# Linear-attention layers reordered: centring folded into TensorE, queries and first feed-forward product split in fp32r, second one in fp32

## What is computed

```python
q = _phi((h @ wq + bq_).reshape(b, s, H, DH))          # _phi(t) = elu(t) + 1, 16 heads of 8
k = _phi((h @ wk + bk_).reshape(b, s, H, DH))
v = (h @ wv + bv_).reshape(b, s, H, DH)
kv = jnp.einsum('bshd,bshm->bhdm', k, v)
z = 1.0 / (jnp.einsum('bshd,bhd->bsh', q, k.sum(axis=1)) + 1e-06)
att = jnp.einsum('bshd,bhdm,bsh->bshm', q, kv, z).reshape(b, s, d)
h = _ln(h + att @ wo + bo_, g1_, be1_)
y = jax.nn.gelu(h @ w1 + c1_, approximate=False) @ w2 + c2_
return _ln(h + y, g2_, be2_)
```

## Time and profile before

| | |
|---|---|
| median of 3 runs | 2228.36 us (2226.25 to 2234.08) |
| the profiled execution | 2234.25 us, span 2232.5 us |
| busy in the span | PE 1889.7 us (85%), DVE 1437.7 (64%), ACT 1330.7 (60%), POOL 533.2 (24%) |
| mean granted TensorE clock | 0.929 of full |
| one layer of stage B | 72.56 us: PE busy 67.57, DVE 38.50, ACT 41.26 |

### The profile page before, as it was taken

How to read it: one execution, slowest core, us unless ns; L and a number is a source line. 1 busy time by engine, 2 the same in 40 slices (tenths; PEclk the granted TensorE clock), 3 DMA queues, 4 the chain that set the end, 5 groups by cost and what they waited for, 6 DMA issues and landing times.

```text
span 2232.5 us, 23751 instructions
## 1 busy us (share of the span) xinstructions
PE 1889.7 (85%) x8305; PEld 1065.8 (48%) x8324; DVE 1437.7 (64%) x2318; ACT 1330.7 (60%) x2118; POOL 533.2 (24%) x525
## 2 busy tenths in 40 slices
PE   8899999999999989899677777997677677777998
PEld 6687444444434437686223233784122222332686
DVE  6687554465445646786755563786899755653787
ACT  6698646465555558797355556555654545565554
POOL 1344000000000001444411113122499501113121
PEclk9899999999999999899779998998799868999899
DMA  2431000000000003321000000210000000000110
GB/s 72 81 76 51 15 17 17 0 17 17 17 0 17 9 10 57 69 69 44 1 1 1 1 1 1 72 34 0 9 4 30 1 1 1 1 1 1 48 57 19
DMA packets 60610, 52.39 MB, mean 23 GB/s; under 512 B 2336, under 2 KB 55968, under 8 KB 60512
## 3 DMA queue, kind: packets, MB, share of 16 engines
q1 hardware_dynamic: 60512, 51.12, 8.9%
HBM read 49.47 MB, written 1.64 MB: 23 GB/s over the span
## 4 chain that ended last, share of the span: by engine, by line
PE 54%; DVE 22%; ACT 15%; issue 5%; DMA 2%; POOL 1%; SPq 0%; ACTq 0%; DVEq 0%; POOLq 0%
PE ps L440 8%; PE ps L442 8%; PE ps L441 8%; PE ps L708 5%; DVE arena L1439 4%; PE ps L225 4%; DVE arena L1184 4%; PE ps L701 4%; PE ps L927 3%; ACT arena L1047 2%; PE ps L897 2%; ACT rstd L242 2%; ACT arena L997 2%; ACT rstd L238 2%; PE ps L886 2%
## 5 line engine op out<-in xcount | busy, mean ns | idle before, releaser
L548 DVE TENSOR_TENSOR hid_lo<-arena,hid_hi 128x512 fp32r<-128x512 f32 x384 | 340.0, 897 | 72.2 <-ACT arena L498 70.2
L1184 DVE TENSOR_REDUCE arena<-ps 128x1 f32<-128x512 f32 (+3 forms) x352 | 214.0, 639 | 90.2 <-PE ps L901 87.4
L526 POOL TENSOR_TENSOR w_lo<-wslot,w_hi 128x512 fp32r<-128x512 f32 x56 | 76.7, 1374 | 787.8 <-DVE w_hi L543 787.8
L1104 POOL TENSOR_SCALAR_AFFINE_SELECT arena<-arena 128x256 f32<-128x256 f32 x256 | 102.5, 406 | 465.4 <-ACT arena L1047 462.8
L440 PE MATMUL ps<-x_hi,w_hi 128*128 128x512 f32 x512 | 208.7, 408 | 2.9 <-POOL w_lo L526 2.2
L441 PE MATMUL ps<-x_lo,w_hi 128*128 128x512 f32 x512 | 205.5, 401 | 0.0
L442 PE MATMUL ps<-x_hi,w_lo 128*128 128x512 f32 x512 | 205.2, 401 | 0.0
L495 ACT ACTIVATE hid_hi<-ps,wslot 128x512 fp32r<-128x512 f32 x256 | 177.1, 692 | 44.9 <-PE ps L442 17.7
L1047 ACT ACTIVATE arena<-ps 128x1024 f32<-128x1024 f32 (+3 forms) x256 | 166.3, 705 | 46.6 <-PE ps L917 45.9
L897 PE MATMUL ps<-arena 128*128 128x128 bf16 (+3 forms) x498 | 134.2, 336 | 63.5 <-DVE arena L1184 35.8
L498 ACT ACTIVATE arena<-ps,wslot 128x512 f32<-128x512 f32 x256 | 175.1, 684 | 16.8 <-DVE hid_lo L548 16.8
(11 more groups left out here) (223 smaller groups left out, 3876.7 us busy)
## 6 DMA issues: line engine op xcount, KB each, us to landing
arena<-gates_dram SPq DMA_DIRECT2D x96, 256.0 KB, 5.1
wslot<-pack_a SPq DMA_DIRECT2D x16, 514.5 KB, 3.6
wslot<-pack_b SPq DMA_DIRECT2D x8, 901.5 KB, 4.6
wslot<-pack_c SPq DMA_DIRECT2D x8, 768.0 KB, 4.6
res<-x_in SPq DMA_DIRECT2D x4, 256.0 KB, 4.4
out_dram<-res SPq DMA_DIRECT2D x4, 256.0 KB, 2.8
bc_dram<-arena SPq DMA_DIRECT2D x1, 384.0 KB, 3.2
arena<-bc_dram SPq DMA_DIRECT2D x16, 24.0 KB
```

The lines of the kernel that those rows point to most:

```text
L548: dve.tensor_tensor(hid_lo[item % 2][:, k, :], hid32[:, k, :], hid_hi[item % 2][:, k, :].bitcast(F32), ALU.subtract).then_inc(S["hid_ok"], 1)
L1184: dve.tensor_reduce(neg_max[:, i, heads[0]:heads[-1] + 1:step], ps[:, bank, 0:len(heads) * keys].rearrange("p (m k) -> p m k", k=keys), AX ...
```

## The change

Stage B is written anew, with the same arithmetic up to rounding.

- **Centring.** A normalization needs h - mean(h). Products with `cent` (identity minus 1/128) put the centred residual right into the PSUM bank in which Wo's or W2's product accumulates, in fp32r from two parts of h (`centred`: `h_hi`, `h_lo`, or `mid_hi`, `mid_lo`). Wo and W2 are centred once per layer by VectorE (`weights`, steps 0 and 1), biases once in all (`c_bias`). So the mean products, the subtraction and the residual addition go. ScalarE squares straight from PSUM (`square`), `var` makes the variance, `root` is Ln and Exp, VectorE scales (`scaled`) and shifts (`shifted`), ScalarE makes the rounded part (`high`), and the remainder is subtracted by GpSimd for the layer's input (`low`) and by VectorE in the middle (`mid_low`).
- **Split products.** Wq and W1 are used as three fp32r products (`split3`). Keys and values stay fp32; `ff2` too, with the gelu's output `hid_g` not split.
- **Attention.** kv is transposed (`kv_t`) and multiplied by Wo beforehand (g), then copied over `kv_bd`; so one product from scaled queries (`qf` times 1/denominator) gives Wo's result. Denominators are folded to 256 columns (two products an item), so the reciprocal is of 128 x 256.
- **Order.** `ff1` uses three banks; the second normalization's `var` of items 0 to 2 stands among the feed-forward products, item 3's after the next layer's first query. The queries and keys/values are interleaved, and keys(b) on VectorE follows keys_values(b). The layers are unrolled. Weight columns are reordered so that Wq and W1 are contiguous; GpSimd makes their remainders in two cuts (256 and 384 columns) for the next layer.

```diff
+hid_g = view(11392, 2, FC, SEQ)
+rz = view(0, 256)
+kv_t, c_bias, w_sum = sb("kv_t", [P, NB, P]), sb("c_bias", [P, 2 * LAYERS]), sb("w_sum", [P, 1 + FC])
+cent_r = sb("cent_r", [P, P], F32R)
+h_hi, h_lo = over("h_hi", "res", 0, [NB, SEQ]), over("h_lo", "xc", 0, [NB, SEQ])
+mid_hi, mid_lo = over("mid_hi", "hb", 0, [NB, SEQ]), over("mid_lo", "arena", 25216, [NB, SEQ])
+wb_hi = [w_hi[0], over("wb_hi1", "arena", 23680, [B_KVB])]
...
+CUTS = [(B_WQ, B_WQ + 2 * P), (B_WQ + 2 * P, B_WO)]
...
+    def split3(bank, w_at, s, hi, lo, lo_ready, stop, start=False):
+        w1, w2 = (t[s][:, w_at:w_at + P] for t in (wb_hi, w_lo))
+        pe.matmul(ps[:, bank, :], w1, hi, start=start, stop=False)
+        pe.matmul(ps[:, bank, :], w2, hi, start=False, stop=False)
+        lo_ready()
+        return pe.matmul(ps[:, bank, :], w1, lo, start=False, stop=stop)
+
+    def centred(bank, hi, lo, stop):
+        pe.matmul(ps[:, bank, :], cent_r[:, :], hi, start=True, stop=False)
+        return pe.matmul(ps[:, bank, :], cent_r[:, :], lo, start=False, stop=stop)
+
+    def var(j, b, bank):
+        pe.wait_ge(S["bsq_ok"], 4 * j + b + 1)
+        pe.matmul(ps[:, bank, :], mean_w, sq[:, b, :], start=True, stop=True).then_inc(S["bvar_mm"], 1)
...
+            split3(b, B_WQ, s, h_hi[:, b, :], h_lo[:, b, :],
+                   lambda: pe.wait_ge(S["h_lo_ok"], m + b + 1), True, True).then_inc(S["q_mm"], 1)
...
+            if b >= 2:
+                pe.wait_ge(S["kv_ok"], m + b - 1)
+            elif l:
+                pe.wait_ge(S["by_ok"], 4 * (j1 - 1) + 2 * b + 2)
...
+        pe.wait_ge(S["w_parts"], c["parts"] + 2 * l + 2)
+        queries(0)
+        if l:
+            last_var(j1 - 1)
+        keys_values(0)
+        queries(1)
+        queries(2)
+        keys_values(1)
+        queries(3)
+        keys_values(2)
+        keys_values(3)
...
+        for b in range(NB):
+            pe.wait_ge(S["kvbd_ok"], m + b + 1)
+            pe.transpose(ps[:, b, 256:256 + P], kv_bd[:, b, :], ident).then_inc(S["kvt_mm"], 1)
+            rows = ps[32 * b:32 * b + 32, 4, 0:256]
+            pe.matmul(rows, ks_h[:, b, 16:48], qf[:, b, 0:256], start=True, stop=False, skip_group_check=True)
+            mm = pe.matmul(rows, ks_h[:, b, 0:32], qf[:, b, 256:512], start=False, stop=True,
+                           skip_group_check=True)
+        mm.then_inc(S["den_mm"], 1)
+        for b in range(NB):
+            pe.wait_ge(S["kvt_ok"], m + b + 1)
+            pe.matmul(ps[:, b, 384:384 + P], kv_t[:, b, :], w[:, B_WO:B_WO + P], start=True,
+                      stop=True).then_inc(S["g_mm"], 1)
...
+        for b in range(NB):
+            pe.wait_ge(S["g_ok"], m + b + 1)
+            centred(b, h_hi[:, b, :], h_lo[:, b, :], False)
+        pe.wait_ge(S["rz_ok"], l + 1)
+        for b in range(NB):
+            for half, spread in enumerate(("spread_a", "spread_b")):
+                mm = pe.matmul(ps[:, 4 + b, 256 * half:256 * half + 256], ccol(spread)[32 * b:32 * b + 32],
+                               rz[32 * b:32 * b + 32, :], start=True, stop=True)
+            mm.then_inc(S["z_bc"], 1)
+        for b in range(NB):
+            pe.wait_ge(S["qz_ok"], m + b + 1)
+            pe.matmul(ps[:, b, :], kv_bd[:, b, :], qf[:, b, :], start=False,
+                      stop=True).then_inc(S["o_mm"], 1)
+        for b in range(NB):
+            var(j1, b, 4 + b)
+
...
+        def ff1(b, k):
+            n = FC * b + k
+            if k == 0:
+                pe.wait_ge(S["mid_hi_ok"], m + b + 1)
+            if n < 3:
+                pe.wait_ge(S["by_ok"], 4 * j1 + n + 1)
+            else:
+                pe.wait_ge(S["gelu_ok"], 16 * l + n - 2)
+            split3(n % 3, B_W1 + k * P, s, mid_hi[:, b, :], mid_lo[:, b, :],
+                   lambda: pe.wait_ge(S["mid_lo_ok"], m + b + 1), True, True).then_inc(S["ff1_mm"], 1)
+
+        def ff2(b, k):
+            if k == 0:
+                centred(4 + b, mid_hi[:, b, :], mid_lo[:, b, :], False)
+            pe.wait_ge(S["gelu_ok"], 16 * l + FC * b + k + 1)
+            mm = pe.matmul(ps[:, 4 + b, :], w[:, B_W2 + k * P:B_W2 + (k + 1) * P], hid_g[:, b % 2, k, :],
+                           start=False, stop=(k == FC - 1))
+            if k == FC - 1:
+                mm.then_inc(S["ff2_mm"], 1)
+
+        for item in range(NB + 1):
+            for k in range(FC):
+                if item < NB:
+                    ff1(item, k)
+                if item:
+                    ff2(item - 1, k)
+                if item == 2 and k == 1:
+                    pe.wait_ge(S["by_ok"], 4 * j1 + 4)
+                    var(j2, 0, LN2_BANK[0])
+                if item == NB and k < 2:
+                    pe.wait_ge(S["gelu_ok"], 16 * l + 14 + k)
+                    var(j2, 1 + k, LN2_BANK[1 + k])
...
+    def square(j, b, bank, done, bias):
+        act.wait_ge(done, 4 * (j // 2) + b + 1)
+        act.activation(sq[:, b, :], ps[:, bank, :], ACT.Square, bias=bias).then_inc(S["bsq_ok"], 1)
+
+    def root(j, b, bank):
+        act.wait_ge(S["bvar_mm"], 4 * j + b + 1)
+        act.activation(rstd[:, b, :], ps[:, bank, :], ACT.Ln, bias=eps).then_inc(S["blog_ok"], 1)
+        act.wait_ge(S["blog_ok"], 4 * j + b + 1)
+        act.activation(rstd[:, b, :], rstd[:, b, :], ACT.Exp, scale=-0.5).then_inc(S["brs_ok"], 1)
+
+    def high(j, b, dst, g, be, done):
+        act.wait_ge(S["by_ok"], 4 * j + b + 1)
+        act.activation(dst[:, b, :], rstd[:, b, :], ACT.Identity, scale=g, bias=be).then_inc(done, 1)
...
+        queries(0)
+        if l:
+            root(j1 - 1, 3, LN2_BANK[3])
+        queries(1)
+        if l:
+            high(j1 - 1, 3, h_hi, before[:, B_G2:B_G2 + 1], before[:, B_BE2:B_BE2 + 1], S["h_hi_ok"])
+        queries(2)
+        keys(0)
+        queries(3)
+        keys(1)
+        keys(2)
+        keys(3)
...
+        for b in range(NB):
+            act.wait_ge(S["kvt_mm"], m + b + 1)
+            act.activation(kv_t[:, b, :], ps[:, b, 256:256 + P], ACT.Copy).then_inc(S["kvt_ok"], 1)
+        act.wait_ge(S["den_mm"], l + 1)
+        act.activation(rz, ps[:, 4, 0:256], ACT.Identity, bias=tiny).then_inc(S["den_ok"], 1)
+        for b in range(NB):
+            act.wait_ge(S["g_mm"], m + b + 1)
+            act.activation(kv_bd[:, b, :], ps[:, b, 384:384 + P], ACT.Copy).then_inc(S["g_ok"], 1)
...
+        for b in range(NB):
+            square(j1, b, b, S["o_mm"], c_bias[:, l:l + 1])
+        g1, be1 = w[:, B_G1:B_G1 + 1], w[:, B_BE1:B_BE1 + 1]
+        for b in range(NB):
+            root(j1, b, 4 + b)
+            if b:
+                high(j1, b - 1, mid_hi, g1, be1, S["mid_hi_ok"])
+        high(j1, NB - 1, mid_hi, g1, be1, S["mid_hi_ok"])
...
+                    act.wait_ge(S["ff2_mm"], m + b - 1)
+                act.activation(hid_g[:, b % 2, k, :], ps[:, (FC * b + k) % 3, :], ACT.Gelu,
+                               bias=w[:, B_C1 + k:B_C1 + k + 1]).then_inc(S["gelu_ok"], 1)
+                if b >= 2 and k == 0:
+                    square(j2, b - 2, 4 + b - 2, S["ff2_mm"], c2)
+        act.preload_act_table_set("natural_log_exp_and_others")
+        square(j2, 2, 6, S["ff2_mm"], c2)
+        root(j2, 0, LN2_BANK[0])
+        root(j2, 1, LN2_BANK[1])
+        high(j2, 0, h_hi, g2, be2, S["h_hi_ok"])
+        root(j2, 2, LN2_BANK[2])
+        high(j2, 1, h_hi, g2, be2, S["h_hi_ok"])
+        square(j2, 3, 7, S["ff2_mm"], c2)
+        high(j2, 2, h_hi, g2, be2, S["h_hi_ok"])
+    root(j2, 3, LN2_BANK[3])
+    high(j2, 3, h_hi, g2, be2, S["h_hi_ok"])
...
+            square_w = wslot[:, s, B_WO:B_KVB].rearrange("p (a n) -> p a n", n=P)
+            dve.tensor_reduce(w_sum[:, :], square_w, AX_X, ALU.add).then_inc(S["w_sum_ok"], 1)
...
+            dve.scalar_tensor_tensor(out=square_w, in0=w_sum[:, :].unsqueeze(2).to_broadcast([P, 1 + FC, P]),
+                                     scalar=-1.0 / P, in1=square_w, op0=ALU.mult,
+                                     op1=ALU.add).then_inc(S["w_mid_ok"], 1)
...
+            dve.tensor_copy(wb_hi[s][:, a:b], wslot[:, s, a:b]).then_inc(S["w_hi_ok"], 1)
...
+    def scaled(j, b, bank, bias):
+        dve.wait_ge(S["brs_ok"], 4 * j + b + 1)
+        dve.scalar_tensor_tensor(out=rstd[:, b, :], in0=ps[:, bank, :], scalar=bias, in1=rstd[:, b, :],
+                                 op0=ALU.add, op1=ALU.mult).then_inc(S["by_ok"], 1)
...
+    def shifted(j, b, dst, g, be, done):
+        dve.wait_ge(S["by_ok"], 4 * j + b + 1)
+        dve.tensor_scalar(dst[:, b, :], rstd[:, b, :], g, be, ALU.mult, ALU.add).then_inc(done, 1)
...
+        queries(0)
+        if l:
+            scaled(j1 - 1, 3, 7, c_bias[:, LAYERS + l - 1:LAYERS + l])
+            shifted(j1 - 1, 3, ha, before[:, B_G2:B_G2 + 1], before[:, B_BE2:B_BE2 + 1], S["h_ok"])
+        queries(1)
+        keys_values(0)
+        queries(2)
+        keys(0)
+        keys_values(1)
+        queries(3)
+        keys(1)
+        keys_values(2)
+        keys(2)
+        keys_values(3)
+        keys(3)
...
```

(106 more changed lines are left out.)

304 lines of the change are left out of this document (144 added, 160 removed).

## The result

The changed kernel takes **2276.18 us** (median of 4 runs, 2273.36 to 2277.43) against 2228.69 (4 runs, 2226.25 to 2234.08) of the kernel before in the same session: ratio **1.0208** (95% interval 1.0187 to 1.0229): slower, well clear of the noise, by about 2%. Predicted were 2265, range 2222 to 2297. The profiled execution took 2275.78 us, span 2274.1, mean granted TensorE clock 0.913.

What follows compares the result with a forecast made beforehand. A layer's second half was taken as bound by TensorE, its first by hand-over latency. Period 71.5 + 4.4 = 75.9 us gave +26 in eight layers, edges +11: 2234 + 26 + 11 = 2271, as median 2265, range 2222 to 2297.

Steps and rivals of the forecast that it cites:

- The likeliest case: Layers of stage B: TensorE's clock falls twice a layer, at the gelu wait and the keys; 2248 to 2284, chance 0.57.
- The walk of a layer: One steady layer followed wait by wait across the engines: period 71.5 us at full clock, 1.1 below before.
- TensorE's work: Products per layer: 27.4 us removed, 19.3 added, so 8.1 less, 65 us in eight layers if nothing waited.
- Denominators in sequence: Attention: a transpose before each item's two products makes them run one after another, 4.4 us; side by side 2.6.
- The clock: After the gelu wait and the keys' waits TensorE drops to half clock, costing 2.3 and 2.1 us a layer.
- Edges: Start and end of stage B: first query +8.6 us later, end +2.7, together +11.
- From profile to median: Whole kernel: the profiled execution lies 6 us above the runs' median, so 2271 becomes 2265.
- Clock up: Rival, layers: the clock stays up, 8 x -1.1 + 11 = +2, 2231 us (2216 with denominators at low bound); chance 0.15.
- Only one fall: Rival, layers: products among the keys' waits suffice, so the clock falls once a layer; 2248 us, chance 0.14.
- Lasting low: Rival: the low clock lasts from keys through denominators, g and spreading into output products; 2297 to 2330, chance 0.12.
- The gelu's table load with a drain behind it: Rival, ScalarE before the gelu: each table load costs about 1.38 us of drain more; 2276 us, chance 0.02.
- The second normalization of items 0 to 2: End of a layer: it lies under TensorE's remaining 6.5 us of work, with high(0) ending at 5.9.

Runs made afterwards that it cites:

- the kernel that has both waits filled: Changed kernel plus products of constant data in TensorE's waits for the first gelu and for keys: 2248.06 us, ratio 1.0066 to the kernel before.
- keys one item later: Changed kernel with keys(b) on VectorE again one item behind keys_values(b): 2232.57 us, ratio 1.0002 to the kernel before.

## Why the prediction was right

The likeliest case came in: slower, with two falls of the clock a layer. The mechanism is the predicted one; that the time came as close as 11 us owes something to luck, since the walk was too short and the falls too dear, the start too long and the end too short. Point by point.

**The walk of a layer** is best compared with the kernel that has both waits filled, since it runs at full clock. From the first output product to the end of the gelu wait 14.7 was predicted and 14.76 measured; from there to `ff1(3,3)` issued 20.7, measured 20.9; from there to the last kv product 26.1, measured 26.8; from there to the next output product 10.0, measured 10.8. Sum 71.5, measured 73.2 in that layer. The largest miss is in the last part: a round of the denominators takes 1.24, not 1.09, which is 0.6 of the 0.8. The first gelu's wait (3.66, "about 4") and the last of the keys' (1.95 against 2.1) were as walked; the first two were 0.8 and 1.2 instead of 1.1 and 1.4. `high` is 0.80 long and holds the next pass back for 0.71, where I had 0.65.

**TensorE's work.** The 8.1 us less did not show in its busy time: at full clock a layer has 61.7 (keys one item later) against 67.57, 5.8 less, because the sum of products left out the denominators, which the walk then has apart.

**Denominators in sequence**, 4.4 a layer: right, 4.9. But my reason, that two products of 256 columns follow each other by their whole time, does not hold: all eight ran in 1.0 us, halves in succession or not, once no transpose stood between. The transpose is the reason, so this price was right by luck.

**The clock.** I had 2.3 + 2.1 = 4.4 a layer, measured 3.5 (76.59 less 73.1). Both places are right. The low level lasted 3.4 us in nine and 6.8 us in four of 13, and the 13 cost 1.9 each on the mean (3.5 x 7 / 13), less than the 2.3 and 2.1 that I charged; and it was missing once.

**Period** 75.9, measured 76.6: a miss of +1.6 in the walk and of -0.9 in the clock. **Layers** +26, measured +32.2. **Edges** +11, measured +12.0: the start +7.5 where I had +8.6, the end +4.5 where I had +2.7. **Sum** +37 for stage B, measured +44.2, and 2.6 less elsewhere.

**From profile to median.** I took the profiled run of before as 6 above its median and carried that over. The changed kernel's profiled run (2275.78) lies at its median (2276.18), so of the 11 us between 2265 and 2276, 6 come from this step and 5 from the terms above. That a profiled run is off its median by some us is a property of that run, not of the kernel.

**The range.** I gave both falls 2248 to 2284 by the bounds of the two prices and of the denominators. Added up, these bounds make 2240 to 2281; the measured 2276 lies in either.

**The rivals.** Clock up: refuted by the rows, and by its price too; even with the clock up the kernel would be slower (73.1 a layer, 2248 measured with the extra products), not the 2231 that I gave it. So the side was not decided by the clock alone. Only one fall: once in seven layers. Lasting low: not seen. The gelu's table load with a drain behind it: 514.87 and 1.28 lead to 516.17 without a gap, as in the earlier trace rows, though 2276 happens to be the number that this rival gave. The second normalization of items 0 to 2 was hidden as walked.

## What to carry to other kernels

Where work is removed from a stretch that is bound by hand-overs, count the waits first: here a layer loses 8.1 us of products and is still about 0.5 longer at full clock. In the layer shown TensorE stands for 11.4 us instead of 5.0, and the denominators with their transposes take 4.9 instead of 1.6; the falls of the clock at the longest waits cost another 3.5. Ask of each engine's written order which instruction stands behind one that must wait for a round trip through another engine; moving three calls by one item was worth 2% of the whole kernel. And keep products of 32 output rows together, with no full-array product between them.
